# Last stage of a graph network on one core: message rows fetched once per step instead of once per tile of edges

## The chip, the core and the metric

The program runs on one core of one Trainium2 chip. The metric is the device time of one execution in microseconds (us), without the profiler. Five engines work side by side: TensorE (PE in the profile, its weight loads PEld), VectorE (DVE), ScalarE (ACT), GpSimd (POOL) and SyncE (SP). [...]

## What is computed

Two graph layers over 6250 nodes of 256 features and 100,000 edges, which come sorted by their target `dst`. Cut to what matters:

```python
h = relu(layernorm(x))
x = x + L0(h, src, dst, ...)          # attention over edges, then an MLP per node
h = relu(layernorm(x))
all_msg = einsum('nf,rfo->rno', h, weight)          # one message per node and relation, 16 relations
msg  = all_msg[rel_type, src] * norm                # one row of 256 per edge
gate = sigmoid(einsum('nf,rf->rn', h, gate_weight[..., 0])[rel_type, src])
agg  = segment_sum(msg * gate[:, None], dst, num_segments=6250)
x = x + relu(agg)
```

The change is about `msg` and `segment_sum`: one row of 256 numbers for each edge is fetched from the table of messages and added to its target node.

## The kernel before

**Stages.** `prepare` computes the steps' tables, q, k and v, and fills the first 221 us. `attention` (to 1710 us) gathers q and v rows edge by edge. `node_mlp` and `messages` (to 2550 us) are the dense part; `messages` writes `msg_d`, 16 rows of 256 per node, already gated. `edge_sum` is the last stage, and `finish` adds x and stores.

**Tiles and steps.** 128 edges make a tile of edges (782 of them, and one of padding, `DENSE` = 783), 128 nodes a tile of nodes (`NODE_TILES` = 49). Since edges are sorted by target, a tile of edges belongs to one tile of nodes, or to two where it spans their border. A **step** is one pair of the two; there are `STEPS` = 832. So a border tile of edges has two steps, one for each tile of nodes.

**The last stage before** (`edge_sum`, L1257 to L1341). The order is written out by hand, unrolled; nothing schedules it.
- GpSimd gathers: for each tile of edges one indirect DMA (L1294) of 128 rows of 1 KB from `msg_d`, by a column of the index table `msg_i`, into a ring of 64 places (`RING`). Before a place is used again it waits for `summed`, the count of finished steps, to be at least e - 64 + 50, because the program doesn't know which steps read the tile. Every fourth gather it waits also for `landed` (L1292).
- SyncE relays landings (L1280 to L1282): the twenty semaphores `got` tell of landings one by one; SyncE waits for each in turn and adds one to `landed`.
- TensorE, for each step (L1302 to L1314): it loads from the table `place` the number of the tile of edges that the step reads, makes the ring's address from it in registers, waits for the one-hot matrix and for `landed` to reach that number (a register's value), and multiplies the one-hot matrix (128x128, float32) with the 128x256 rows. The load is issued two steps ahead. In the profile one such multiplication is two matmuls.
- VectorE, for each step: the one-hot matrix (L1326), which holds the edge's weight where the target matches, in a ring of four; and the addition of the step's product to `sums` (L1339), two steps later, at an address that it loads eight at a time from `place` (L1331).

**The index table.** `prepare` finds for each step its tile of edges by a product: `cols` holds src, dst, relation and weight of the edges (columns n = 0 to 3 in that order, each with two PSUM banks), `sel` selects. The line L748 does it in seven chunks c of edge tiles, for n = 0, 1 and 3. The message index 16 * src + relation was made on the columns before the product (L427), for tiles of edges, and seven transposes (L756) turn it into `msg_i` (L451, L452). `src_i`, which the attention stage uses, is by step.

Of the kernel before, what the change touches and what calls it, by code (L numbers as in the profile page):

```python
# [20 lines left out]
I32 = mybir.dt.int32  # L21
U16 = mybir.dt.uint16
U_ROUND = float(3 * 2 ** 22)
ALU = mybir.AluOpType
# [3 lines left out]
P = 128  # L28
# [61 lines left out]
def gnn_program(nc, x, src, dst, rel, norm, wqkv, bqkv, g_attn, b_attn, g_res, b_res,  # L90
# [17 lines left out]
    msg_i_d = dram("msg_i_d", [P, EDGE_TILES_PAD], I32)  # L108
    tab_d = dram("tab_d", [ROUNDS, TABLE], U16)

    with ExitStack() as whole:
# [35 lines left out]
        msg_i = sb(last, "msg_i_again", [P, EDGE_TILES_PAD], I32)  # L147
# [47 lines left out]
def prepare(nc, sb, ps, sem, x, src, dst, rel, norm, wqkv, bqkv, g_attn, b_attn, iota_n, ident, ident_b, part, ones,  # L195
# [20 lines left out]
    with ExitStack() as ctx:  # L216
        dloc = sb(ctx, "dloc", [P, STEPS])
        norm_s = sb(ctx, "norm_s", [P, STEPS])
        msg_i = sb(ctx, "msg_i", [P, EDGE_TILES_PAD], I32)
# [78 lines left out]
        with nc.Block() as block:  # L298
            @block.vector
            def _(dve):  # L300
# [121 lines left out]
                for c in range(ICN):  # L422
                    if c >= 2:
                        dve.wait_ge(sel_free, c - 1)
                    if c == 2:
                        dve.wait_ge(split, 3)
                        nc.vector.scalar_tensor_tensor(out=cols[:, 2], in0=cols[:, 0], scalar=float(RELS), in1=cols[:, 2],  # L427
                                                       op0=ALU.mult, op1=ALU.add).then_inc(split, 1)
# [21 lines left out]
                at["src"] = signal(last)  # L450
                nc.vector.tensor_copy(msg_i[:, 0:4 * IC], pb[4][:, 0:4 * IC])  # L451
                at["msg"] = signal(nc.vector.tensor_copy(msg_i[:, 4 * IC:], pb[5][:, 0:(ICN - 4) * IC]))  # L452
# [255 lines left out]
            def _(pe):  # L708
# [34 lines left out]
                for c in range(ICN):  # L743
                    pe.wait_ge(dve_did, at["sel", c])
                    for n in (0, 1, 3):
                        for h in range(2):
                            for part_of in (cols_hi, cols_lo):
                                mm = nc.tensor.matmul(pb[2 * n + h][:, 0:SH], part_of[:, n, c, :],  # L748
                                                      sel[:, c % 2, h * SH:(h + 1) * SH],
                                                      start=(c == 0 and part_of is cols_hi),  # L750
                                                      stop=(c == ICN - 1 and part_of is cols_lo))
                    mm.then_inc(sel_free, 1)
                    if c == ICN - 3:
                        pe.wait_ge(split, 4)
                        for d in range(ICN):
                            nc.tensor.transpose(pb[4 + d // 4][:, d % 4 * IC:(d % 4 + 1) * IC], cols[:, 2, d], ident[0:IC, 0:IC])  # L756
# [500 lines left out]
def edge_sum(nc, sb, ps, sem, table, sums, iota_n, late, place, msg_i, idx_ld, late_ld, x1_d, x1_all, got):  # L1257
# [3 lines left out]

    before = [16 * len([n for n in range(STEPS) if n % SLOTS // 2 == b]) for b in range(len(got))]
    BANKS = 4
    HOTS = 4
    RING = 64
    x1_ld, hot_ok, summed, acc_ok, zero_ok, landed = (
        sem(f"rel_{n}") for n in ("x1", "hot", "sum", "acc", "zero", "landed"))
    with ExitStack() as ctx:
        dloc, norm_s = late[:, 0], late[:, 1]
        rows = sb(ctx, "rel_rows", [P, RING * FEAT])  # L1270
# [3 lines left out]
        with nc.Block() as block:  # L1274
            @block.sync
            def _(sp):
                for g in range(GROUPS):
                    sp.dma_start(x1_all[:, g], x1_d.rearrange("(g t p) f -> g p t f", t=GROUP, p=P)[g]).then_inc(x1_ld, 16)
                for e in range(DENSE):
                    b = e % len(got)  # L1280
                    sp.wait_ge(got[b], before[b] + 16 * (e // len(got) + 1))
                    sp.sem_inc(landed, 1)  # L1282
                sp.wait_ge(x1_ld, 16 * GROUPS)

            @block.gpsimd
            def _(pool):
                pool.wait_ge(idx_ld, 16)
                for e in range(DENSE):
                    if e >= RING:
                        pool.wait_ge(summed, e - RING + NODE_TILES + 1)  # L1290
                    if e >= len(got) and e % 4 == 0:
                        pool.wait_ge(landed, e - len(got) + 4)  # L1292
                    at = (e + 1) % RING * FEAT
                    nc.gpsimd.indirect_dma_start(rows[:, at:at + FEAT], None, table,  # L1294
                                                 bass.IndirectOffsetOnAxis(ap=msg_i[:, e:e + 1], axis=0)
                                                 ).then_inc(got[e % len(got)], 16)

            @block.tensor
            def _(pe):
                def edge_of(n):  # L1300
                    r, s = n // UNROLL, n % UNROLL
                    return nc.values_load_multi_w_load_instructions(  # L1302
                        place[r:r + 1, s:s + 1], engines=[mybir.EngineType.PE], min_val=1, max_val=DENSE,
                        skip_runtime_bounds_check_because="the tile of edges that a step reads, counted from one")[1][0]

                pe.wait_ge(late_ld, 48)
                ahead = [edge_of(0), edge_of(1)]
                for n in range(STEPS):
                    edge = ahead.pop(0)
                    at = nc.s_assert_within(pe.snap(edge & (RING - 1)) * FEAT, 0, (RING - 1) * FEAT,  # L1310
                                            skip_runtime_bounds_check_because="the remainder of a division by the ring's length")
                    pe.wait_ge(hot_ok, n + 1)
                    pe.wait_ge(landed, edge)
                    nc.tensor.matmul(sum_ps[n % BANKS][:], hot[:, n % HOTS, :], rows[:, bass.ds(at, FEAT)],  # L1314
                                     start=True, stop=True).then_inc(summed, 1)
                    if n + 2 < STEPS:
                        ahead.append(edge_of(n + 2))
# [704 lines left out]
```

## Time and profile before

| | us |
|---|---|
| median of 3 timed runs | 3281.6 |
| lowest, highest | 3278.4, 3282.5 |
| the profiled execution, its own span | 3773.2 |
| first stage ends | 221.4 |
| attention ends | 1710 |
| messages are done, first gather of the last stage | 2550 |
| last addition ends | 3748.4 |

The profile is of one execution, recorded by the hardware; its span is the time that it knows of it, and no other time of that execution is given. "Busy" is time in which an engine executes. Idle time is put down to what released the engine: an instruction of another engine, a DMA, or "issue", where the profile shows nothing that was waited for. Register, branch and semaphore instructions are of an engine's sequencer (PEldq, SPq, DVEq) and don't count as busy. PEclk is the granted TensorE clock, 1.00 for 2.4 GHz.

### The profile page before, as it was taken

What the parts mean: (1) busy time and instruction counts of PE and PEld (TensorE: products, weight loads), DVE (VectorE), ACT (ScalarE), POOL (GpSimd) and SP (SyncE); (2) the same over time, 40 slices, a digit from 0 to 9 for tenths busy, and PEclk for the clock granted to TensorE, in tenths of its full rate; (3) what the DMA queues carried; (4) which work ended last, traced back from release to release, by engine and by line L of the source; (5) the groups of instructions that cost most, each with busy time, mean ns of one, the idle gap of its engine ahead of it and who ended that gap; (6) DMA issues with size and microseconds to landing.
All of it is one profiled execution on the core that took longest, in us unless ns stands there. A gap on an engine that the chain in (4) does not pass through costs nothing. (4 is left out here: it accounts for less than half of the span.)

```text
span 3773.2 us, 52431 instructions
## 1 busy us (share of the span) xinstructions
PE 2896.0 (77%) x13207; PEld 1940.5 (51%) x13207; DVE 2133.7 (57%) x4604; ACT 963.3 (26%) x2525; POOL 1732.1 (46%) x1863
## 2 busy tenths in 40 slices
PE   6838888888888888869999999992655555555555
PEld 4525555555555555549998888871333333333332
DVE  6727776677767777768862222222544444444446
ACT  3513333333333333346663333330000000000000
POOL 2555655555555555433300000006466666666661
PEclk9968998899989999979999999995867677776678
DMA  4455666666666666533345444445233333333332
GB/s 151 147 166 164 196 192 193 181 192 189 194 188 190 192 191 195 160 114 99 99 136 210 187 186 188 187 178 164 69 91 92 92 92 92 91 91 92 92 92 88
DMA packets 233908, 557.07 MB, mean 148 GB/s; under 512 B 48498, under 2 KB 128454, under 8 KB 221095
## 3 DMA queue, kind: packets, MB, share of 16 engines
q0 software_dynamic: 104144, 324.24, 30.4%
q1 hardware_dynamic: 108463, 193.61, 14.1%
q10 hardware_dynamic: 21032, 35.85, 3.2%
q8 instruction: 141, 2.31, 0.2%
q14 instruction: 128, 1.05, 0.1%
HBM read 402.87 MB, written 150.71 MB: 147 GB/s over the span
## 5 line engine op out<-in xcount | busy, mean ns | idle before, releaser
L1294 POOL DMA_INDIRECT rel_rows<-msg_d,msg_i_again x783 | 743.3, 949 | 976.8 <-ACTq L1274 571.7
L1314 PE MATMUL rel_ps<-rel_rows,rel_hot 128*128 x1664 | 678.5, 538 | 525.0 <-issue 364.4
L873 POOL DMA_INDIRECT qv_rows<-qv_d,src_i x832 | 798.4, 960 | 567.6 <-PE out_ps L1155 354.2
L1314 PEld LDWEIGHTS rel_ps<-rel_rows,rel_hot 128*128 128x128 f32 x1664 | 367.1, 254 | 836.5 <-issue 806.3
L1339 DVE TENSOR_TENSOR sums_all<-sums_all,rel_ps 128x256 f32 x832 | 350.4, 421 | 630.4 <-PE rel_ps L1314 247.0
L1155 PE MATMUL out_ps<-qv_rows,hot 128*128 128x264 f32 x1664 | 635.8, 467 | 44.8 <-DVE qv_rows L950 25.0
L1031 ACT COPY at_acc<-out_ps 128x264 f32 x832 | 310.3, 380 | 726.9 <-PE out_ps L1155 581.1
L1110 PE MATMUL kx<-k,hot_t 128*128 x2496 | 398.4, 297 | 64.4 <-issue 48.4
L896 DVE TENSOR_TENSOR qv_rows<-qv_rows,kx 128x512 f32<-128x512 f32 x416 | 278.7, 679 | 204.4 <-remote 121.6
L1957 PE MATMUL up_hid_ps<-up_split,ms_hTs 128*128 128x512 f32 x1416 | 347.5, 396 | 0.0
L1110 PEld LDWEIGHTS kx<-k,hot_t 128*128 128x128 bf16 x2496 | 252.9, 105 | 175.4 <-issue 108.6
L1155 PEld LDWEIGHTS out_ps<-qv_rows,hot 128*128 128x128 f32 x1664 | 277.3, 209 | 87.1 <-issue 63.7
L1326 DVE TENSOR_SCALAR rel_hot<-iota_n,late 128x128 f32<-128x128 f32 x832 | 297.2, 357 | 0.1
L1957 PEld LDWEIGHTS up_hid_ps<-up_split,ms_hTs 128*128 128x128 f32 x1416 | 264.7, 189 | 59.9
L1165 PEld LDWEIGHTS out_ps<-at_zero 1*128 1x128 bf16 x832 | 76.2, 92 | 377.9 <-issue 366.0
L950 DVE TENSOR_TENSOR qv_rows<-qv_rows,p_ps 128x1056 f32<-128x1056 f32 x208 | 250.5, 1246 | 0.4 <-PE p_ps L1144 0.3
L901 DVE TENSOR_REDUCE sc<-qv_rows 128x32 f32<-128x1024 f32 x208 | 248.3, 1215 | 1.8
L1957 PE MATMUL up_out_ps<-up_split,ms_hTs 128*128 128x512 f32 x936 | 233.6, 397 | 0.0
L1165 PE MATMUL out_ps<-at_zero 1*128 1x8 bf16 x832 | 145.8, 175 | 108.1 <-issue 61.8
L1957 PEld LDWEIGHTS up_out_ps<-up_split,ms_hTs 128*128 128x128 f32 x936 | 174.9, 189 | 39.5
L1736 PE MATMUL up_out_ps<-wout,up_split 128*128 128x256 f32 x1176 | 154.8, 290 | 22.8 <-DVE up_x_h L1503 22.7
L1736 PEld LDWEIGHTS up_out_ps<-wout,up_split 128*128 128x128 f32 x1176 | 147.5, 196 | 26.0 <-DVE up_x_h L1503 15.0
(213 smaller groups left out, 2883.3 us busy)
## 6 DMA issues: line engine op xcount, KB each, us to landing
msg_d<-up_x SPq DMA_DIRECT2D x33, 1024.0 KB, 3.9
msg_d<-up_gelu SPq DMA_DIRECT2D x33, 1024.0 KB, 3.8
msg_d<-up_res SPq DMA_DIRECT2D x32, 1024.0 KB, 3.8
dl_b<-dlt_d ACTq DMA_DIRECT2D x50, 512.0 KB
qv_rows<-qv_d,src_i POOLq DMA_INDIRECT x832
rel_rows<-msg_d,msg_i_again POOLq DMA_INDIRECT x783
qv_d<-qv SPq DMA_DIRECT2D x6, 1820.0 KB, 7.2
agg_d<-at_acc SPq DMA_DIRECT2D x49, 132.0 KB
```

Source lines behind the costliest of these rows:

```text
L873: nc.gpsimd.indirect_dma_start(rows[:, n % SLOTS, :], None, qv_d, bass.IndirectOffsetOnAxis(ap=src_i[:, n:n + 1], axis=0)).then_inc(got[n ...
L896: nc.vector.tensor_tensor(q, q, kx[i % 2][:], ALU.mult).then_inc(prod_ok, 1)
L950: nc.vector.tensor_tensor(v, v, weights.to_broadcast([P, QUAD, HEADS, HW]), ALU.mult).then_inc(val_ok, 1)
L1031: nc.scalar.copy(acc[:, at:at + AGGW], out_ps[:, bass.ds(banks[s % QUAD], AGGW)]).then_inc(acc_ok, 1)
L1110: last = nc.tensor.matmul(kx[i % 2][:, b, :], hot_t[:, k % HOT_RING, s * P:(s + 1) * P], k_flat[:, bass.ds(tiles[s] * KW + n * FEAT, FEAT) ...
L1155: nc.tensor.matmul(out_ps[:, bass.ds(bank, AGGW)], hot[:, s, :], rows[:, slot(k, s), FEAT:], start=False, stop=True, skip_group_check=True ...
L1294: nc.gpsimd.indirect_dma_start(rows[:, at:at + FEAT], None, table, bass.IndirectOffsetOnAxis(ap=msg_i[:, e:e + 1], axis=0)).then_inc(got[e ...
L1314: nc.tensor.matmul(sum_ps[n % BANKS][:], hot[:, n % HOTS, :], rows[:, bass.ds(at, FEAT)], start=True, stop=True).then_inc(summed, 1)
L1326: nc.vector.tensor_scalar(hot[:, n % HOTS, :], iota_n[:], dloc[:, n:n + 1], norm_s[:, n:n + 1], ALU.is_equal, ALU.mult).then_inc(hot_ok, 1)
L1339: nc.vector.tensor_tensor(sums[:, bass.ds(here, FEAT)], sums[:, bass.ds(here, FEAT)], sum_ps[n % BANKS][:], ALU.add).then_inc(acc_ok, 1)
L1736: last = nc.tensor.matmul(out_ps[n_t % 2], hid[:, a, m, t * P:(t + 1) * P], wout[:, b, m, :], start=(i == 0), stop=(i == len(parts) - 1))
L1957: last = nc.tensor.matmul(mm_ps[m % BANKS][:], hTs[:, n % 2, a, k, :], wrel[:, c, b, k], start=(i == 0), stop=(i == len(parts) - 1))
```

## The change

Rows are gathered for each step instead of each tile of edges: 832 gathers in place of 783, so that step n reads place n % 40. The ring has 40 places with one semaphore per two, as in the attention stage. GpSimd waits for `summed` to be n - 39. SyncE's relay and the semaphore `landed` go. TensorE waits for two gathers before every second step, with fixed numbers, and loads nothing and computes no address. The index is now made by step: L748 also chooses the relation (n = 2, its high part alone, since it is a small whole number), and 16 * src + relation is made afterwards by VectorE from `src_i`. The transposes and the multiplication at L427 go. VectorE's part of the last stage, its load of places included, and the table `place` stay.

```diff
--- before.py
+++ after.py
@@ -105,7 +105,7 @@
     hb_d = dram("hb_d", [STEPS, P])
     fl_d = dram("fl_d", [ICN * HEADS, 2 * FLAGS])
     late_d = dram("late_d", [2, P, STEPS])
-    msg_i_d = dram("msg_i_d", [P, EDGE_TILES_PAD], I32)
+    msg_i_d = dram("msg_i_d", [P, STEPS], I32)
     tab_d = dram("tab_d", [ROUNDS, TABLE], U16)
 
     with ExitStack() as whole:
...
@@ -422,10 +422,6 @@
                 for c in range(ICN):
                     if c >= 2:
                         dve.wait_ge(sel_free, c - 1)
-                    if c == 2:
-                        dve.wait_ge(split, 3)
-                        nc.vector.scalar_tensor_tensor(out=cols[:, 2], in0=cols[:, 0], scalar=float(RELS), in1=cols[:, 2],
-                                                       op0=ALU.mult, op1=ALU.add).then_inc(split, 1)
                     at["sel", c] = did(nc.vector.tensor_scalar(sel[:, c % 2], edge_tile[0:IC, :], part_c[0:IC, c:c + 1], None,
                                                                ALU.is_equal))
                     if c == 1:
@@ -447,9 +443,12 @@
                 dve.wait_ge(pe_did, 5)
                 for h in range(2):
                     last = nc.vector.tensor_copy(src_i[:, h * SH:(h + 1) * SH], pb[h][:, 0:SH])
-                at["src"] = signal(last)
-                nc.vector.tensor_copy(msg_i[:, 0:4 * IC], pb[4][:, 0:4 * IC])
-                at["msg"] = signal(nc.vector.tensor_copy(msg_i[:, 4 * IC:], pb[5][:, 0:(ICN - 4) * IC]))
+                at["src"] = did(last)
+                for h in range(2):
+                    a, b = h * SH, (h + 1) * SH
+                    last = nc.vector.scalar_tensor_tensor(out=msg_i[:, a:b], in0=src_i[:, a:b], scalar=float(RELS),
+                                                          in1=pb[4 + h][:, 0:SH], op0=ALU.mult, op1=ALU.add)
+                at["msg"] = signal(last)
                 for h in range(2):
                     a, b = h * SH, (h + 1) * SH
                     last = nc.vector.scalar_tensor_tensor(out=dloc[:, a:b], in0=node_tile[:, a:b], scalar=-float(P),
@@ -742,18 +741,15 @@
                 pe.wait_ge(split, 3)
                 for c in range(ICN):
                     pe.wait_ge(dve_did, at["sel", c])
-                    for n in (0, 1, 3):
+                    for n in range(4):
+                        parts_of = (cols_hi,) if n == 2 else (cols_hi, cols_lo)
                         for h in range(2):
-                            for part_of in (cols_hi, cols_lo):
+                            for i, part_of in enumerate(parts_of):
                                 mm = nc.tensor.matmul(pb[2 * n + h][:, 0:SH], part_of[:, n, c, :],
                                                       sel[:, c % 2, h * SH:(h + 1) * SH],
-                                                      start=(c == 0 and part_of is cols_hi),
-                                                      stop=(c == ICN - 1 and part_of is cols_lo))
+                                                      start=(c == 0 and i == 0),
+                                                      stop=(c == ICN - 1 and i == len(parts_of) - 1))
                     mm.then_inc(sel_free, 1)
-                    if c == ICN - 3:
-                        pe.wait_ge(split, 4)
-                        for d in range(ICN):
-                            nc.tensor.transpose(pb[4 + d // 4][:, d % 4 * IC:(d % 4 + 1) * IC], cols[:, 2, d], ident[0:IC, 0:IC])
                 pe.wait_ge(sel_free, ICN)
                 pe.sem_inc(pe_did, 1)
 
@@ -1259,15 +1255,15 @@
 
 
 
+    PER = 2
+    RING = PER * len(got)
     before = [16 * len([n for n in range(STEPS) if n % SLOTS // 2 == b]) for b in range(len(got))]
     BANKS = 4
     HOTS = 4
-    RING = 64
-    x1_ld, hot_ok, summed, acc_ok, zero_ok, landed = (
-        sem(f"rel_{n}") for n in ("x1", "hot", "sum", "acc", "zero", "landed"))
+    x1_ld, hot_ok, summed, acc_ok, zero_ok = (sem(f"rel_{n}") for n in ("x1", "hot", "sum", "acc", "zero"))
     with ExitStack() as ctx:
         dloc, norm_s = late[:, 0], late[:, 1]
-        rows = sb(ctx, "rel_rows", [P, RING * FEAT])
+        rows = sb(ctx, "rel_rows", [P, RING, FEAT])
         hot = sb(ctx, "rel_hot", [P, HOTS, P])
         sum_ps = [ps(ctx, f"rel_ps{i}", [P, FEAT]) for i in range(BANKS)]
 
@@ -1276,45 +1272,27 @@
             def _(sp):
                 for g in range(GROUPS):
                     sp.dma_start(x1_all[:, g], x1_d.rearrange("(g t p) f -> g p t f", t=GROUP, p=P)[g]).then_inc(x1_ld, 16)
-                for e in range(DENSE):
-                    b = e % len(got)
-                    sp.wait_ge(got[b], before[b] + 16 * (e // len(got) + 1))
-                    sp.sem_inc(landed, 1)
                 sp.wait_ge(x1_ld, 16 * GROUPS)
 
             @block.gpsimd
             def _(pool):
                 pool.wait_ge(idx_ld, 16)
-                for e in range(DENSE):
-                    if e >= RING:
-                        pool.wait_ge(summed, e - RING + NODE_TILES + 1)
-                    if e >= len(got) and e % 4 == 0:
-                        pool.wait_ge(landed, e - len(got) + 4)
-                    at = (e + 1) % RING * FEAT
-                    nc.gpsimd.indirect_dma_start(rows[:, at:at + FEAT], None, table,
-                                                 bass.IndirectOffsetOnAxis(ap=msg_i[:, e:e + 1], axis=0)
-                                                 ).then_inc(got[e % len(got)], 16)
+                for n in range(STEPS):
+                    if n >= RING:
+                        pool.wait_ge(summed, n - RING + 1)
+                    nc.gpsimd.indirect_dma_start(rows[:, n % RING, :], None, table,
+                                                 bass.IndirectOffsetOnAxis(ap=msg_i[:, n:n + 1], axis=0)
+                                                 ).then_inc(got[n % RING // PER], 16)
 
             @block.tensor
             def _(pe):
-                def edge_of(n):
-                    r, s = n // UNROLL, n % UNROLL
-                    return nc.values_load_multi_w_load_instructions(
-                        place[r:r + 1, s:s + 1], engines=[mybir.EngineType.PE], min_val=1, max_val=DENSE,
-                        skip_runtime_bounds_check_because="the tile of edges that a step reads, counted from one")[1][0]
-
-                pe.wait_ge(late_ld, 48)
-                ahead = [edge_of(0), edge_of(1)]
                 for n in range(STEPS):
-                    edge = ahead.pop(0)
-                    at = nc.s_assert_within(pe.snap(edge & (RING - 1)) * FEAT, 0, (RING - 1) * FEAT,
-                                            skip_runtime_bounds_check_because="the remainder of a division by the ring's length")
+                    if n % PER == 0:
+                        b = n % RING // PER
+                        pe.wait_ge(got[b], before[b] + 16 * PER * (n // RING + 1))
                     pe.wait_ge(hot_ok, n + 1)
-                    pe.wait_ge(landed, edge)
-                    nc.tensor.matmul(sum_ps[n % BANKS][:], hot[:, n % HOTS, :], rows[:, bass.ds(at, FEAT)],
+                    nc.tensor.matmul(sum_ps[n % BANKS][:], hot[:, n % HOTS, :], rows[:, n % RING, :],
                                      start=True, stop=True).then_inc(summed, 1)
-                    if n + 2 < STEPS:
-                        ahead.append(edge_of(n + 2))
 
             @block.vector
             def _(dve):
```

TensorE in the last stage, two steps of before and five of now. `rel_ps` is the bank of the product, `rel_rows` the ring, `rel_hot` the one-hot matrix; `rel_landed` is the relay's count, `got` counts landings. Before:

```order
L1302 TENSOR_LOAD place
L1314 REGISTER_ALU [waits rel_landed,rel_hot]
L1314 ISA
L1314 MATMUL rel_ps3<-rel_rows,rel_hot 128x256
L1302 TENSOR_LOAD place
L1314 REGISTER_ALU [waits rel_landed,rel_hot]
L1314 ISA
L1314 MATMUL rel_ps0<-rel_rows,rel_hot 128x256
```

Now:

```order
L1294 MATMUL rel_ps1<-rel_rows,rel_hot 128x256 [waits rel_hot]
L1294 MATMUL rel_ps2<-rel_rows,rel_hot 128x256 [waits rel_hot,got17]
L1294 MATMUL rel_ps3<-rel_rows,rel_hot 128x256 [waits rel_hot]
L1294 MATMUL rel_ps0<-rel_rows,rel_hot 128x256 [waits rel_hot,got18]
L1294 MATMUL rel_ps1<-rel_rows,rel_hot 128x256 [waits rel_hot]
```

The register load and the two register instructions of each step are gone, and their waits stand at the matmul itself, with a landing's semaphore at every second one.

GpSimd at the start of the last stage, before (the pattern of one gather with the wait for `landed` and three without goes on, from the 65th gather on with `rel_sum` at every one):

```order
L1285 UNCONDITIONAL_BRANCH [waits barrier_Pool_Activation_PE_DVE_SP_gather]
L1294 DMA rel_rows<-msg_d,msg_i_again 128x256 [waits rel_idx]
L1294 DMA rel_rows<-msg_d,msg_i_again 128x256 x19
L1294 DMA rel_rows<-msg_d,msg_i_again 128x256 [waits rel_landed]
L1294 DMA rel_rows<-msg_d,msg_i_again 128x256 x3
L1294 DMA rel_rows<-msg_d,msg_i_again 128x256 [waits rel_landed]
L1294 DMA rel_rows<-msg_d,msg_i_again 128x256 x3
```

Now:

```order
L1277 UNCONDITIONAL_BRANCH [waits barrier_Pool_Activation_PE_DVE_SP_gather]
L1283 DMA rel_rows<-msg_d,msg_i_again 128x256 [waits rel_idx]
L1283 DMA rel_rows<-msg_d,msg_i_again 128x256 x39
L1283 DMA rel_rows<-msg_d,msg_i_again 128x256 [waits rel_sum] x792
L1270 UNCONDITIONAL_BRANCH
```

40 gathers start without a wait for the sums, then each of the other 792 waits for `rel_sum`; no gather waits for `rel_landed`.

## Rows read from the trace of the kernel before

**Rows 1.** Busy time by stage; columns stand in the first row.

```profile
core 0: us, PE busy (x) PEld busy (x) DVE busy (x) ACT busy (x) POOL busy (x), PEclk, DMA share, GB/s
0.00:221.40 221.40, 175.77 (x605) 107.12 (x605) 153.62 (x479) 100.80 (x255) 89.34 (x131) 0.96 0.44 144
221.40:1710.00 1488.60, 1210.12 (x6609) 752.39 (x6610) 1038.73 (x1697) 500.92 (x1382) 836.48 (x877) 0.89 0.64 181
1710.00:2550.00 840.00, 831.56 (x4331) 713.89 (x4329) 361.72 (x757) 361.60 (x889) 63.03 (x73) 1.00 0.43 166
2550.00:3748.50 1198.50, 678.51 (x1664) 367.10 (x1664) 565.87 (x1665) 0.00 (x0) 743.28 (x783) 0.71 0.32 92
```

**Rows 2.** The page: costliest groups of the last stage.

```profile
L1294 POOL DMA_INDIRECT rel_rows<-msg_d,msg_i_again x783 | 743.3, 949 | 976.8 <-ACTq L1274 571.7
L1314 PE MATMUL rel_ps<-rel_rows,rel_hot 128*128 x1664 | 678.5, 538 | 525.0 <-issue 364.4
...
L1339 DVE TENSOR_TENSOR sums_all<-sums_all,rel_ps 128x256 f32 x832 | 350.4, 421 | 630.4 <-PE rel_ps L1314 247.0
...
L1326 DVE TENSOR_SCALAR rel_hot<-iota_n,late 128x128 f32<-128x128 f32 x832 | 297.2, 357 | 0.1
```

**Rows 3.** One line, the gather (L1294): durations (ns min/median/max), idle time by releaser.

```profile
L1294 POOL DMA_INDIRECT rel_rows<-msg_d,msg_i_again x783: 943/949/1037, 2550.1 to 3697.5; - x196
...
  issue: 194.0, 554
  PE rel_ps L1314: 132.6, 175
  remote: 76.0, 50
```

**Rows 4.** Timeline, start of the gathers (start us, us, engine, line, idle before).

```profile
2550.05 1.04 POOL L1294 DMA_INDIRECT rel_rows<-msg_d,msg_i_again  x1 [571.73 <-ACTq L1274]
2551.39 0.95 POOL L1294 DMA_INDIRECT rel_rows<-msg_d,msg_i_again  x1 [0.30 <-issue]
...
2552.65 0.95 POOL L1294 DMA_INDIRECT rel_rows<-msg_d,msg_i_again  x1 [0.30 <-issue]
```

**Rows 5.** Timeline, GpSimd alone, end of the gathers.

```profile
3696.22 0.95 POOL L1294 DMA_INDIRECT rel_rows<-msg_d,msg_i_again  x1 [0.31 <-issue]
3697.48 0.95 POOL L1294 DMA_INDIRECT rel_rows<-msg_d,msg_i_again  x1 [0.30 <-issue]
```

**Rows 6.** One line, the matmuls (L1314) and their register work, whole stage.

```profile
L1314 PEldq ALU_OP  x832: 2/32/1384, 2565.1 to 3746.8; - x167
```

**Rows 7.** The same line, 3700 to 3750 us alone, no gather left.

```profile
L1314 PE MATMUL rel_ps<-rel_rows,rel_hot x116: 379/392/478, 3699.8 to 3747.3; 128*128 x116
L1314 PEldq ALU_OP  x57: 32/32/32, 3700.3 to 3746.8; - x57
```

**Rows 8.** SyncE, the relay (L1282), 2565 to 3697 us.

```profile
L1282 SPq EVENT_SEMAPHORE  x780: 3/17/711, 2565.0 to 3696.4; - x195
```

**Rows 9.** VectorE, the places loaded every eighth step (L1331).

```profile
L1331 DVEq TENSOR_LOAD <-place x104: 1823/1876/1941, 2562.8 to 3741.5; - x104
```

**Rows 10.** The page: gathers of the attention stage.

```profile
L873 POOL DMA_INDIRECT qv_rows<-qv_d,src_i x832 | 798.4, 960 | 567.6 <-PE out_ps L1155 354.2
```

**Rows 11.** First stage, the choosing matmuls (L748).

```profile
L748 PE MATMUL prep_ps<-sel,cols_hi x42: 352/352/684, 28.6 to 47.5; 112*128 112x416 f32 x42
```

**Rows 12.** Timeline of the first stage, the transposes and what follows.

```profile
42.64 0.83 PE L756 MATMUL prep_ps<-ident,k 112*128 112x112 f32 x7
...
47.48 0.35 PE L748 MATMUL prep_ps<-sel,cols_hi 112*128 112x416 f32 x1
...
47.67 0.35 PE L748 MATMUL prep_ps<-sel,cols_lo 112*128 112x416 f32 x1
...
49.15 0.61 DVE L451 CAST msg_i<-prep_ps 128x448 int32<-128x448 f32 x1
...
49.68 0.50 DVE L452 CAST msg_i<-prep_ps 128x336 int32<-128x336 f32 x1
```

More of the change, by code:

```diff
@@ L146, in gnn_program @@
         last = whole.enter_context(ExitStack())
-        msg_i = sb(last, "msg_i_again", [P, EDGE_TILES_PAD], I32)
+        msg_i = sb(last, "msg_i_again", [P, STEPS], I32)
         late = sb(last, "late", [P, 2, STEPS])
@@ L218, in prepare @@
         norm_s = sb(ctx, "norm_s", [P, STEPS])
-        msg_i = sb(ctx, "msg_i", [P, EDGE_TILES_PAD], I32)
+        msg_i = sb(ctx, "msg_i", [P, STEPS], I32)
         dlt = sb(ctx, "dlt", [P, ICN, P], BF16)
```

## The prediction

> **What bounds the kernel now.** First the busy time by stage [rows 1]: the last stage takes 1198.5 us of the 3773.2 us span. In it GpSimd is busy 743.3 us, TensorE 678.5 us and VectorE 565.9 us: no engine is full, so a wait or an overhead sets the pace. The stage before it has TensorE busy 831.6 of 840.0 us, and there is no slack in it. Then the page's groups [rows 2]: 783 gathers of 949 ns, 1664 matmuls (two a step, 832 steps), 832 additions of 421 ns and 832 one-hots of 357 ns.
>
> The gather's own line [rows 3] has some 405 us idle between gathers. Part of it comes with every gather: where nothing holds GpSimd up, gathers still start 1.25 us apart, 0.95 us busy and 0.30 us not [rows 4, 5]. That is 235 us over 782 gaps. From 2550.05 to 3697.48 us are 1147.4 us, 782 x 1.25 are 977.5; so **170 us** are waits. Who made them? When the last gather starts at 3697.5 us, 116 matmuls, 58 steps, are still to come [rows 5, 7], and they take 47.5 us, 0.82 us a step, with the granted clock high. GpSimd had run as far ahead as its ring lets it: in this execution TensorE was behind, not the gathers. Yet with no gather running its step is 0.82 us, far below the 1.25 us of a gather. What slows it beside gathers is in its register work: an operation that takes 32 ns each time in the last 47 us [rows 7] takes up to 1384 ns over the stage [rows 6], and SyncE's relay goes from 17 to 711 ns at its worst [rows 8].
>
> **Profiled and unprofiled time.** The span is 3773.2 us, the median of the runs is 3281.6: 491.6 us less. So stretches of this trace do not exist at that length in a timed run, and the question of this case is which. The third stage is packed and can give nothing [rows 1]. If the last stage took its 1198.5 us in a timed run too, the first would have to give up all its 45.6 us without a matmul (221.4 - 175.8) and the attention stage nearly all the 449.9 us in which VectorE is not busy (1488.6 - 1038.7): 495.5 in sum, against 491.6 wanted. No stage with chains of waits runs that tight. I conclude that the last stage gives up a good part. The natural part is the 170 us: register and semaphore operations that stretch many times over, on two engines, only while gathers run, look like the recording of events in a crowd, not like work.
>
> **The change part by part, in a timed run.**
> - Gathers: 832 instead of 783, since a tile of edges that spans two node tiles is fetched twice. If the gathers set the pace, it costs 49 periods. GpSimd's busy time alone gives 49 x 0.949 = 46.5 us, the lower bound; the whole period gives 49 x 1.25 = 61.3 us, the upper one, if the 0.30 us are real. Nothing in the trace tells how much of the 0.30 us a timed run keeps; I take the middle, **+54 us**. The attention gathers have the same durations [rows 10]. The transfers grow by 6% from a DMA share of 0.32 [rows 1]: nothing. The Trainium skill, page "DMA: Bandwidth & Descriptors", section "Anatomy of one DMA — SWDGE (gpsimd) path", calls descriptor generation small, with many descriptors to be had before it shows; by that the 49 gathers would cost nothing. The trace speaks against it: each holds GpSimd for 949 ns.
> - TensorE loses a register load, two register operations and a wait in every step, and SyncE loses 784 relays. Their cover is the gather: 0.82 us a step with all of them [rows 7] against 0.949 us at least for a gather. Removed, they are worth nothing while gathers set the pace; without that cover they are worth the 170 us and what follows from them.
> - The ring. GpSimd is no longer held 14 steps behind (64 less 50) but always 40, and doesn't wait for landings. The first gather starts at 2550.05 us and TensorE's first register operation at 2565.1 us [rows 4, 6]; landing takes less than that, 12 gathers. 40 cover it. TensorE now waits for pairs: at most one more gather, 1.25 us, once. After the last gather I allow 5 us for landing, two matmuls and an addition: 0, as before.
> - VectorE still loads its places from a table every eighth step, 1.88 us each [rows 9]. It is unchanged and its pace is in the 0.82 us.
> - First stage: 14 more choosing matmuls at 0.19 us apart [rows 12] (their own 352 ns overlap [rows 11]) are +2.7 us; seven transposes go, -0.8 us [rows 12]. VectorE's two operations that make the message index stay two, 0.61 and 0.50 us, now reading src_i as well; one multiplication further up goes and was hidden. All this lies before the first products: **+2 us**, between 0 and +4.
>
> Sum: +54 + 2 = **+56 us**, 3281.6 + 56 = 3337.6 us. Against the profiled execution the sum is another one, and shows what I mean: 831 x 1.25 = 1038.8 after 2550.05, 5 behind it, ends the stage at 3593.9 in place of 3748.5, with +2 a span near **3621 us**. I expect the profile's span to fall by about 150 us while the time rises.
>
> **The rivals.**
> 1. Faster: the stretched operations are real. Mechanism: TensorE's and SyncE's register and semaphore operations become slow while gathers run, the ring fills, GpSimd waits. The change takes most of them away. In full that gives 3281.6 - 155 + 2 = 3128.6 us. For it: all 170 us stand in the trace, and TensorE is idle for "issue" [rows 2]. Against it: the account of the 491.6 us above. A share s of it gives 56 - 209 s us, no change at s = 0.27 (46 us of real waits), 3233 at half. In a sentence of its own: the Trainium skill, "Runtime: NRT & Kernel Launch", section "The launch sequence", gives profile and run a gap of about 6 us whatever the kernel, by which the stretches would be real and this rival right; here the gap is 491.6 us, so the trace does not bear the rule out. Chance 0.28.
> 2. No change: a timed gather is shorter than VectorE's and TensorE's 0.82 us a step, in profile and out of it. Then the 49 gathers are hidden and 3284 us result. Against it: it needs 949 ns of busy time to shrink by 14% while VectorE's doesn't. This also covers a cancelling share of rival 1. Chance 0.11.
> 3. Slower than forecast: the 40 deep ring or pairs make TensorE wait at its landings; by one 1.25 us for each time the ring starts cold, so a few us. It widens the upper end only.
>
> That the change doesn't do what it says can be left out: its gathers and their addresses are fixed numbers.
>
> **How the numbers follow.** Forecast, gathers set the pace: 0.61, all of it slower; its own range is 3327 (46.5 and 0 less 1) to 3350 (61.3, 4 and a few us of rival 3). Rival 2: 0.11 within 0.2% (6.6 us, about what a measurement of this kernel tells from no change). Rival 1: 0.28 faster. The range takes in the forecast, rival 2 and rival 1 down to half its price, 3233, and a little below: 3230 to 3350.
>
> **What would show it.** In the profile after: 832 gathers starting 1.25 us apart with hardly a longer gap, the last one near 3589 us; GpSimd at 66% or more of the stage; TensorE waiting for landed rows; no 700 ns stretches on TensorE; a stage of some 1044 us. Those would hold with a rise or a fall of the time. What tells them apart is the time alone: below 3275 us the register work was a real bound. If gathers in the new profile still wait for TensorE, the reading of the stretched operations is wrong.

## The result and the profile after

The change makes the kernel **slower: 3340.64 us** (4 runs, 3338.56 to 3342.85) against 3280.49 us before, a ratio of 1.0185 with a 95% interval of 1.0173 to 1.0197, or +60.2 us. The forecast was 3337.6 us.

The trace shown ahead of the prediction can't be understood without one fact, which the experiments brought out: the kernel before takes near 3280 us in some series of runs and near 3800 us in others, steadily within each, and its recorded execution of 3773.2 us was of the second kind, its timed runs of the first ("at 3280" and "at 3800" below; each difference is taken within one series).

Busy time by stage of the kernel after, at 3280 (columns as in [rows 1]):

```profile
0.00:219.90 219.90, 171.98 (x612) 105.72 (x612) 153.10 (x478) 100.91 (x255) 89.03 (x130) 0.98 0.45 145
219.90:1425.00 1205.10, 1109.78 (x6604) 710.48 (x6605) 1025.48 (x1696) 503.44 (x1381) 831.58 (x877) 0.96 0.76 224
1425.00:2265.70 840.70, 832.21 (x4336) 714.54 (x4335) 362.38 (x758) 362.27 (x891) 63.60 (x74) 1.00 0.44 166
2265.70:3313.60 1047.90, 758.45 (x1664) 435.17 (x1664) 574.66 (x1664) 0.00 (x0) 789.49 (x832) 0.63 0.38 111
```

The last stage takes 1047.9 us; the attention stage's gathers end at 1298 us where they ended at 1584 in the trace before, at 3800, in code that the change does not touch. The page's groups (as [rows 2]):

```profile
L1283 POOL DMA_INDIRECT rel_rows<-msg_d,msg_i_again x832 | 789.5, 949 | 825.1 <-ACTq L1270 571.7
L1294 PE MATMUL rel_ps<-rel_rows,rel_hot 128*128 128x256 f32 x1664 | 758.6, 603 | 295.3 <-DMA rel_rows<-msg_d,msg_i_again 271.1
...
L1317 DVE TENSOR_TENSOR sums_all<-sums_all,rel_ps 128x256 f32 x832 | 350.4, 421 | 471.3 <-PE rel_ps L1294 460.9
...
L1304 DVE TENSOR_SCALAR rel_hot<-iota_n,late 128x128 f32<-128x128 f32 x832 | 294.6, 354 | 0.1
```

And the gather's own line (as [rows 3]; the last row is the time from a gather's start to its landing):

```profile
L1283 POOL DMA_INDIRECT rel_rows<-msg_d,msg_i_again x832: 945/949/1037, 2265.7 to 3307.6; - x167
...
  issue: 143.0, 469
  PE rel_ps L1294: 110.4, 362
...
DMA to landing us min/median/max: 2.6/2.7/6.2
```

832 gathers lie between 2265.7 and 3307.6 us: 1041.9 us over 831 gaps, 1.254 us each. The idle time of 143.0 and 110.4 us is 253.4 in all, 0.305 us a gap: nothing but the 0.30 us that come with each gather. Not one gap is long. A row lands 2.7 us after its gather starts. The timeline of the end shows who waits for whom now:

```profile
3305.08 0.94 POOL L1283 DMA_INDIRECT rel_rows<-msg_d,msg_i_again  x1 [0.30 <-PE rel_ps L1294]
...
3305.34 2.08 PE L1294 MATMUL rel_ps<-rel_rows,rel_hot 128*128 128x256 f32 x4 [0.44 <-DMA rel_rows<-msg_d,msg_i_again]
...
3306.33 0.94 POOL L1283 DMA_INDIRECT rel_rows<-msg_d,msg_i_again  x1 [0.30 <-issue]
...
3307.58 0.95 POOL L1283 DMA_INDIRECT rel_rows<-msg_d,msg_i_again  x1 [0.30 <-PE rel_ps L1294]
...
3311.65 2.07 PE L1294 MATMUL rel_ps<-rel_rows,rel_hot 128*128 128x256 f32 x4 [1.01 <-DMA rel_rows<-msg_d,msg_i_again]
...
3313.86 0.42 DVE L1317 TENSOR_TENSOR sums_all<-sums_all,rel_ps 128x256 f32 x1 [0.43 <-PE rel_ps L1294]
```

TensorE waits for landed rows ("DMA" as the releaser) and works four matmuls, two steps, at a time, as the pairs of its waits have it; 6.7 us pass from the last gather's start to the end of the last addition. I had allowed 5.

### The profile page after: what moved, and what is told of

It reads as the page before. It is cut to its first block and busy times, and to the rows that moved or that the text cites. A ratio compares the mean times of both kernels' runs of the same rounds, so it can differ in the third digit from the quotient of the medians.

```text
span 3336.8 us, 48617 instructions
## 1 busy us (share of the span) xinstructions
PE 2872.5 (86%) x13214; PEld 1965.9 (59%) x13214; DVE 2129.7 (64%) x4603; ACT 966.6 (29%) x2525; POOL 1773.7 (53%) x1912
## 5 line engine op out<-in xcount | busy, mean ns | idle before, releaser
L1283 POOL DMA_INDIRECT rel_rows<-msg_d,msg_i_again x832 | 789.5, 949 | 825.1 <-ACTq L1270 571.7
L1294 PE MATMUL rel_ps<-rel_rows,rel_hot 128*128 128x256 f32 x1664 | 758.6, 603 | 295.3 <-DMA rel_rows<-msg_d,msg_i_again 271.1
L1294 PEld LDWEIGHTS rel_ps<-rel_rows,rel_hot 128*128 128x128 f32 x1664 | 435.2, 289 | 618.4 <-DMA rel_rows<-msg_d,msg_i_again 527.3
L1151 PE MATMUL out_ps<-qv_rows,hot 128*128 128x264 f32 x1664 | 590.1, 437 | 33.0 <-DVE qv_rows L946 18.5
L1106 PE MATMUL kx<-k,hot_t 128*128 x2496 | 354.4, 278 | 13.2 <-DVE hot_t L885 7.3
L1151 PEld LDWEIGHTS out_ps<-qv_rows,hot 128*128 128x128 f32 x1664 | 251.6, 191 | 75.7 <-issue 54.3
L1106 PEld LDWEIGHTS kx<-k,hot_t 128*128 128x128 bf16 x2496 | 235.4, 98 | 99.0 <-issue 37.6
```

The lines of the kernel that those rows point to most:

```text
L1106: last = nc.tensor.matmul(kx[i % 2][:, b, :], hot_t[:, k % HOT_RING, s * P:(s + 1) * P], k_flat[:, bass.ds(tiles[s] * KW + n * FEAT, FEAT) ...
L1151: nc.tensor.matmul(out_ps[:, bass.ds(bank, AGGW)], hot[:, s, :], rows[:, slot(k, s), FEAT:], start=False, stop=True, skip_group_check=True ...
L1283: nc.gpsimd.indirect_dma_start(rows[:, n % RING, :], None, table, bass.IndirectOffsetOnAxis(ap=msg_i[:, n:n + 1], axis=0)).then_inc(got[n ...
```

## The experiments

All edits are to the kernel before, but for E5. Two series came at 3280 (that of the result and that of E7, E8 and E9), three at 3800 (E1 to E4; E5 and E6; E10 to E12). The record has chip 4 beside E5 and E6 at 3800 and beside E7 to E9 at 3280, so the chip's number alone doesn't tell which it will be.

**E1, before once more.** No edit.

> The kernel before, unchanged, recorded once more. Two accounts of the 491.6 us between its span and its timed runs. Theory A: that one recording was disturbed (a property of the execution, not of the kernel): now the span is near 3280 us, the attention stage some 284 us shorter as in the profile of the change, and the gathers of the last stage start 1.25 us apart all through. Theory B: recording this kernel always stretches its register work: the span is again above 3600 us and TensorE's register operations again take up to 1400 ns.

It fell at 3800: the recorded execution took 3791.84 us, its own span 3790.0 of them, beside a median of 3800.7 for runs of the same kernel. So a recorded execution is a timed one, 1.8 us longer than its span. The other runs, at 3280 and at 3800, have spans on record too, 1.8 to 1.9 us shorter than their times: recording stretched nothing. What theory B foresaw came (a span of 3790.0 us, a register operation of 1421 ns), but not for its reason, and theory A was wrong. The 491.6 us lie between two conditions in which the kernel runs, and in the slow one each execution has them. Stages and gathers are as in the trace ahead of the prediction:

```profile
0.00:217.50 217.50, 172.06 (x605) 105.03 (x605) 153.91 (x479) 100.81 (x255) 89.40 (x131) 0.98 0.45 147
217.50:1720.00 1502.50, 1219.81 (x6661) 757.03 (x6662) 1045.02 (x1717) 505.54 (x1395) 837.40 (x882) 0.89 0.63 180
1720.00:2552.00 832.00, 823.54 (x4279) 706.28 (x4277) 354.12 (x738) 355.51 (x876) 59.51 (x70) 1.00 0.44 167
2552.00:3764.50 1212.50, 672.30 (x1664) 372.48 (x1664) 564.69 (x1664) 0.00 (x0) 741.49 (x783) 0.71 0.31 91
```

```profile
L1294 POOL DMA_INDIRECT rel_rows<-msg_d,msg_i_again x783: 940/946/1036, 2552.0 to 3713.2; - x196
...
  issue: 192.9, 549
  PE rel_ps L1314: 134.1, 176
  remote: 88.9, 52
```

**E2 and E10, the first stage alone.**

```diff
+++ prepare as in the change, msg_i [P, STEPS]; edge_sum as before, reading msg_i[:, e]
```

> The first stage of the change, with the last stage of before. The rows of the last stage are chosen by the wrong column of the index, so the messages added are not those of the reference; the amount of work is the same. My step for the first stage was +2 us, 0 to +4. If it holds, this kernel is 0 to 4 us slower than before, and the last stage alone answers for 56 to 60 of the 60.1 us. A rival: the waits behind the choosing products (src_i, then the index, then the first products) cost 8 us or more, and the gathers correspondingly less.

> The first stage of the change with the last stage of before (the wrong column of the index is read, so the messages added are not those of the reference; the amount of work is the same). In the profile of the change the first gather of the last stage starts at 2265.7 us, in those of before's front 2263.8 and 2264.9. My step was +2 us; a rival is 0, its cover being the wait for loads. Where before takes near 3280 us I expect +1 to +4 us, close to what five rounds can tell. Its last stage is that of before, so its profile shows before's gathers on such a chip: 1.25 us apart, none longer.

Both came at 3800: -0.5 us (0.9995, interval 0.9983 to 1.0007) and +3.5 us (1.0007, 0.9994 to 1.0021). By the times the first stage costs nothing that can be told; 8 us or more at once are not excluded by the second alone (its interval ends at +8.0), but are by the first (+2.7). The traces tell more. The last choosing matmul starts at 47.67 us in the trace before [rows 12] and here in the change:

```profile
48.66 0.34 PE L748 MATMUL prep_ps<-sel,cols_lo 112*128 112x416 f32 x1
```

That is +0.99 us in one pair of executions, and executions of the same first stage differ by up to 1.9 us at this point. The fourteen traces together are clearer. From the first to the last choosing matmul pass 17.9 to 19.4 us in the ten with the first stage of before (18.7 in the mean) and 20.1 to 21.1 in the four with that of the change (20.6): +1.9 us. The first gather of the attention stage starts 2.0 us later in the mean, at 220.8 in place of 218.8 us, though single ones overlap there.

**E3, E6 and E11, no register work on TensorE.**

```diff
-                    edge = ahead.pop(0)
-                    at = nc.s_assert_within(pe.snap(edge & (RING - 1)) * FEAT, ...
+                    edge = min(DENSE, n + 1 - n * NODE_TILES // STEPS)
+                    at = edge % RING * FEAT
```

> The kernel before with TensorE's table load, registers and address left out: the tile of edges that a step reads is a fixed number spread evenly over the steps, so some steps read a neighbouring tile and the sums are not the reference's. 783 gathers, SyncE's relay and the ring stay. If the gathers set the pace, the time is that of before within 4 us (at most the few us that before loses to waits). If the register work was a bound that the change removed, this kernel is clearly faster than before, by 20 us or more.

> The kernel before with TensorE's table load, registers and address left out, some steps reading a neighbouring tile, as once before; there it was 16 us faster where before took 3800 us, with 79 of 782 gaps between gathers still long. Where before takes near 3280 us: gathers set the pace, so it is 0 to 4 us faster. If register work were the bound, 20 us or more.

> The kernel before without TensorE's table load, registers and register address (some steps read a neighbouring tile), a third time, for a chip on which before takes near 3280 us; on the other it gained 16 to 18 us. If gathers set the pace it gains nothing, under 4 us. If register work is a bound in part, 10 us or more.

All three came at 3800: -16.3 us (ratio 0.9959, 0.9946 to 0.9973), -17.9 (0.9957, 0.9939 to 0.9974) and -13.8 (0.9958, 0.9946 to 0.9971). That is between the two marks of the expectation (4 and 20 us). So there the register work has a price, a tenth of the waits. Most of them stay without it: 167 us of 782 gaps beyond 1.254 us in E3, as many as in the trace before (167) and 14 less than in E1 (181). And yet no step's matmul is late in E3: none starts more than 0.43 us after its one-hot is made and the second matmul of the step before has started, where in the trace before 198 of 830 start more than 0.5 us after that. What makes GpSimd wait must be sought elsewhere (E5). At 3280 this edit was not tried. E8 answers for it from the other side.

**E4 and E7, 49 more gathers.**

```diff
+                    if e % 16 == 8:
+                        if e > 8:
+                            pool.wait_ge(spare_ld, 16 * (e // 16))
+                        nc.gpsimd.indirect_dma_start(spare[:], None, table, ...).then_inc(spare_ld, 16)
```

> The kernel before with 49 more gathers, one behind every sixteenth, of rows that nobody reads; nothing waits for them but the end. If the gathers set the pace and the 0.30 us between them are real, +61 us (49 x 1.25), as much as the whole change. If only the 0.949 us of busy time are paid, +46. If the gathers were hidden behind 0.82 us steps, 0 to 10 us.

> The kernel before with 49 more gathers of rows that nobody reads, once more (60.7 us where before took 3800 us). Where before takes near 3280 us: +61 us if gathers set the pace with their whole 1.25 us period, +46 if only the 0.949 us of busy time count, 0 to 10 us if they are hidden behind TensorE's register work.

At 3800 +60.7 us (1.0164, 1.0151 to 1.0178), at 3280 +65.5 us (1.0194, 1.0180 to 1.0208). E7 adds as many gathers as the change (and a wait behind each, long met) and nothing else of it, and gets the change's whole loss. At 3800 the waits stay beside the added gathers (185 us in E4 and 181 in E1 beyond 1.254 us a gap). The extra gather (L1302) stands in the row of the others with the same 1.25 us (timeline, GpSimd alone, E7):

```profile
2275.01 0.94 POOL L1296 DMA_INDIRECT rel_rows<-msg_d,msg_i_again  x1 [0.30 <-issue]
2276.26 0.95 POOL L1302 DMA_INDIRECT rel_spare<-msg_d,msg_i_again  x1 [0.30 <-issue]
2277.51 0.95 POOL L1296 DMA_INDIRECT rel_rows<-msg_d,msg_i_again  x1 [0.30 <-issue]
```

Rival 2, gathers hidden behind 0.82 us steps, falls with this: 65.5 us for 49 are 1.34 us each, a little over the period of 1.25. So does, for gathers like these, what the Trainium skill says on the page "DMA: Bandwidth & Descriptors", section "Anatomy of one DMA — SWDGE (gpsimd) path", that many descriptors can be made before their cost shows.

**E5, the change once more**, beside before.

> The change, unaltered, beside the kernel before on the same chip. Where before takes near 3280 us: 3340 us, +60, with gathers 1.25 us apart. Where before takes near 3800 us, as in the last four comparisons, two theories part. Theory A: what is slow there is TensorE's and SyncE's supply of instructions while gathers run; the change takes SyncE's 784 relays and half of TensorE's instructions away, its gathers come 1.25 us apart again, and it is 100 us or more faster than before. Theory B: something else is slow there, which the change leaves; then the 170 us of waits stay and the change is about 60 us slower there too.

It came at 3800: 3807.37 us against 3798.73, +8.6 us (1.0025, 1.0012 to 1.0037). Neither theory: the change wins most of its gathers back there, but not the 170 us. The gather's line:

```profile
L1283 POOL DMA_INDIRECT rel_rows<-msg_d,msg_i_again x832: 940/946/1037, 2563.3 to 3750.6; - x167
...
  issue: 171.0, 541
  PE rel_ps L1294: 160.3, 247
  remote: 69.7, 43
```

832 gathers take 1187.3 us; over 1.254 a gap that leaves 145 us of waits, where the trace before has 167 and E1 181 by the same count. Its timeline shows what they are made of:

```profile
3007.14 0.42 DVE L1317 TENSOR_TENSOR sums_all<-sums_all,rel_ps 128x256 f32 x1 [2.88 <-PE rel_ps L1294]
3007.48 0.34 DVE L1304 TENSOR_SCALAR rel_hot<-iota_n,late 128x128 f32<-128x128 f32 x1
3007.66 0.98 POOL L1283 DMA_INDIRECT rel_rows<-msg_d,msg_i_again  x1 [0.30 <-issue]
...
3007.87 1.22 PE L1294 MATMUL rel_ps<-rel_rows,rel_hot 128*128 128x256 f32 x2 [2.27 <-issue]
3008.94 0.94 POOL L1283 DMA_INDIRECT rel_rows<-msg_d,msg_i_again  x1 [0.30 <-issue]
3011.36 0.42 DVE L1317 TENSOR_TENSOR sums_all<-sums_all,rel_ps 128x256 f32 x1 [3.54 <-remote]
3011.50 0.94 POOL L1283 DMA_INDIRECT rel_rows<-msg_d,msg_i_again  x1 [1.61 <-remote]
3011.70 0.34 DVE L1304 TENSOR_SCALAR rel_hot<-iota_n,late 128x128 f32<-128x128 f32 x1
...
3012.18 1.19 PE L1294 MATMUL rel_ps<-rel_rows,rel_hot 128*128 128x256 f32 x2 [3.09 <-DVE rel_hot L1304]
3014.19 0.42 DVE L1317 TENSOR_TENSOR sums_all<-sums_all,rel_ps 128x256 f32 x1 [2.16 <-PE rel_ps L1294]
3014.33 0.94 POOL L1283 DMA_INDIRECT rel_rows<-msg_d,msg_i_again  x1 [1.90 <-PE rel_ps L1294]
```

TensorE is not late here. Its pairs of matmuls start at 3007.87 and 3012.18 us, 0.05 and 0.14 us after their one-hots are made, and over the whole stage none starts more than 0.43 us late, counted as in E3. Late is the sign that a step is finished. Counted in order, the addition at 3011.36 is that of step 275 (the first is 0). By the trace the two matmuls of this step ended at 3003.67; such ends are modelled, but those of steps 276 and 277 had started by 3007.87. 379 of 830 additions start more than 0.5 us after their product and VectorE's work before it, by up to 5.2 us; in the change at 3280 it is 83, by up to 1.7 us, beside 104 loads of places. GpSimd sees the same: its gather at 3011.50 waits for the same step 275 in the same count `summed`, and starts 0.14 us after the addition, as the gather at 3014.33 does after the addition of step 276. Of the 90 gathers from the 41st on that start after more than 0.6 us of idle time, 86 start 0.14 us after the addition of their step, 4.3 us in the median after its product. In the trace before it is 87 of 92.

So at 3800 the count that TensorE raises with its matmuls is seen microseconds late, by two engines at the same moment, and the one-hots, which VectorE makes behind its additions, and TensorE's next matmuls come late in consequence. This is so with register operations on TensorE and without. Whether the matmul ends late or its signal does, and why, is open. That the gathers themselves slow it fits the end of the stage [rows 7], where they are over, but no run took them away.

**E8 and E9, more register work on TensorE.**

```diff
-                        ahead.append(edge_of(n + 2))
+                        ahead.append([edge_of(n + 2) for _ in range(2)])       # E9: range(4)
...
+                    for other in more:
+                        pe.wait_ge(hot_ok, other)
```

> The kernel before with TensorE's work on registers enlarged: two table loads for each step instead of one, and one more wait on the value, which is always met. In 3700 to 3750 us of the profile of before a step takes 0.82 us with one load; a second of 0.29 us plus a wait of 0.05 makes at most 1.16 us. A step has 783 x 1.25 / 832 = 1.18 us. If gathers set the pace where before takes 3280 us: no change, under 7 us. If register work is a bound: +250 us at the most (832 x 0.3), over 50 in any case. Where before takes 3800 us, TensorE's instructions are slow beside gathers, and it is slower by 50 us or more.

> The same with four table loads for each step. One load takes 0.29 us and a wait 0.05: a step of TensorE's takes 0.68 to 0.82 us plus 3 x 0.34, so 1.7 to 1.84 us against the 1.18 us of the gathers. The cover is gone and TensorE sets the pace: +430 to +550 us. If loads overlap each other, less: with 0.1 us a load, it stays below 1.18 us and costs nothing.

Both at 3280. E8 (the loads double, and one more wait that is always met): 3276.04 us against 3277.27, -1.2 us (0.9996, 0.9987 to 1.0005), no change. With twice the loads of before nothing is lost. It is also the best picture of before at 3280 that I have, since its 783 gathers and its relay are those of before. First the last stage (columns as in [rows 1]), then the gather's line, then a register operation of TensorE's:

```profile
2263.80:3249.50 985.70, 730.72 (x1664) 319.45 (x1664) 587.85 (x1665) 0.00 (x0) 742.28 (x783) 0.77 0.38 112
```

```profile
L1294 POOL DMA_INDIRECT rel_rows<-msg_d,msg_i_again x783: 942/947/1037, 2263.8 to 3243.4; - x196
...
  issue: 188.3, 618
  PE rel_ps L1316: 49.1, 161
```

```profile
L1316 PEldq ALU_OP  x832: 32/32/32, 2278.8 to 3247.1; - x167
```

783 gathers from 2263.8 to 3243.4 us are 979.6 us, 1.253 us a gap. No gap is long, and 32 ns are 32 ns at minimum, median and maximum (in E7 too, with TensorE's code as before), against 2 to 1384 in [rows 6]. The last stage takes 985.7 us, 62.2 less than the change's.

E9: 3843.59 us, +566.3 us (1.1724, 1.1708 to 1.1740), a little over the 430 to 550 expected. Four loads of 0.29 us each do not overlap (one step's start at 3000.22, 3000.58, 3000.93 and 3001.29 us), and now GpSimd waits for TensorE. First the gather's line, then the loads:

```profile
L1294 POOL DMA_INDIRECT rel_rows<-msg_d,msg_i_again x783: 940/944/1036, 2264.7 to 3699.6; - x196
...
  PE rel_ps L1316: 654.5, 697
...
  issue: 31.8, 79
```

```profile
L1302 PEldq TENSOR_LOAD <-place x3328: 280/290/320, 2264.1 to 3814.0; - x196
```

The matmuls' 832 steps lie between 2279.9 and 3816.2 us, 1.85 us a step. The gathers' cover for TensorE ends somewhere between two and four loads.

**E12, half the rows.**

```diff
-                    nc.gpsimd.indirect_dma_start(rows[:, at:at + FEAT], None, table, ... ap=msg_i[:, e:e + 1]
+                    nc.gpsimd.indirect_dma_start(rows[0:64, at:at + FEAT], None, table, ... ap=msg_i[0:64, e:e + 1]
```

> The kernel before, each gather of the last stage fetching 64 rows instead of 128 (the other half of the ring is zeroed once, so half of the messages are left out of the sums). It measures what the 1.25 us consist of. Theory A: the 0.95 us are written per row and the 0.30 us per gather: period 0.78 us, then VectorE's and TensorE's 0.82 us a step are the bound, the stage takes 832 x 0.82 = 682 instead of 980 us, 300 us faster. Theory B: the whole is per gather: no change. Where before takes 3800 us the gain of A is smaller.

At 3800: +2.8 us (1.0012, 0.9998 to 1.0025). The time can't tell much there, since waits fill what is saved (GpSimd is idle 454 us between gathers, 421 in E1), but the row can:

```profile
L1294 POOL DMA_INDIRECT rel_rows<-msg_d,msg_i_again x783: 892/899/982, 2558.1 to 3717.2; - x196
```

899 ns for 64 rows, 946 for 128 (E1): 47 ns for 64 rows, and by an estimate along this line some 850 that come with every gather. Theory A is wrong, B nearly right.

## Why the prediction was right, and where its reasoning was not

- **Gathers set the pace in a timed run** (forecast 0.61): right, at 3280. Every gap is 1.25 us in the change and in E8, and TensorE waits for landings.
- **49 gathers, 46.5 to 61.3 us, taken as 54**: the upper end was the true one. 49 x 1.254 are 61.4, and the 0.30 us between gathers are real, as all of the span is (E1). The middle was no evidence; E7 has 65.5. I also weighed the Trainium skill's small price of descriptors (the page and section named at E4 and E7) against the 949 ns of the row and took the row, rightly.
- **Register load, registers and relay worth nothing under that cover**: right at 3280; E8 doubles the load for -1.2 us. (SyncE's relays are 783, not 784.) At 3800 the registers alone are worth 14 to 18 us (E3, E6, E11).
- **First stage, +2 us**: borne out by the traces, +1.9 us for the choosing products as in the sum (2.7 - 0.8) and 2.0 to the first gather; E2 and E10 don't tell it from 0.
- **Sum**: 61.4 + 1.9 = 63.3 us against 60.2 measured, whose interval is 56.8 to 64.6. My 56 was short by the part of the gathers' period that I left out.
- **The account of the 491.6 us**: the step that failed. I set it down to the recording, where the two came from different conditions (E1). The Trainium skill, page "Runtime: NRT & Kernel Launch", section "The launch sequence", has a gap of about 6 us, the same for every kernel, by which the profile's time is the longer. That it doesn't depend on the kernel agrees: it is 1.8 to 1.9 us in every run here. Its size and sign don't agree: here the run is longer than the span (3338.56 against 3336.8), though the page's total may take in more than the span. So the stretches were real in their execution, as I had said the rule would have it. That the last stage is shorter in the timed runs, which I had worked out from the 491.6 us, was right (985.7 us in E8 against 1198.5), and so the waits rightly got no price; the reason I gave for them was wrong. That this did no harm was luck: the change was measured in the same series as the timed runs at 3280 (three of the result's four runs of before are those ahead of the prediction), while at 3800 the difference is +8.6 us (E5), and nothing in my reasoning foresaw that.
- **What slows TensorE's step beside gathers**: I put it on the register work. Without that work most of the waits stay (E3), and the late count of finished steps is there in E5 without a register operation on TensorE.
- **The profile of the change**: forecast near 3621 us of span, last gather at 3589; it has 3336.8 and 3307.6. The stage's length was forecast as 1044 us and is 1048. The rest is the attention stage, which in the other condition gathers at 1.64 us a step instead of 1.30.
- **Rival 1** (0.28): wrong at 3280; at 3800 nearly what I had priced as its break-even. There the change keeps +61.4 us of gathers. Beside the trace before it gets back 22 us of waits (167 - 145) and 17 behind the last gather (to the end of the last addition 51.0 us before, 33.6 after), +22 us in the stage. Beside E1 it is 35 and 18 us, +8 in the stage. These are single executions; the measured difference of the medians is +8.6. A kernel judged in that condition alone would have been called the same.

No run tried a version that might beat both. At 3280, with the register work hidden, before already gathers as few tiles as there are, at the pace of the gathers.

## What to carry to other kernels

Compare the recorded execution with the timed runs before reading it. Where they differ by more than a few us, look for unchanged stages that run at another pace, and record again before any sum. A queue of indirect gathers is priced by their number: here 1.25 us each with 128 rows, and some 50 ns less with 64; keep their count low and let other engines pay in registers, as long as a step of theirs stays below the gathers' period. To find out how much register work fits under such a cover, add some: one load more cost nothing, three cost 566 us.

## What the hardware showed that I had not expected

- The same kernel takes 3277 to 3281 us in some series and 3799 to 3801 in others (medians), a factor of 1.16. Gathers and VectorE's operations keep their durations. In stages with gathers TensorE's register and SyncE's semaphore operations of 17 to 46 ns take up to 1.4 us (E1), and the count of finished steps is seen late, by up to 5.2 us at the additions, by VectorE and GpSimd at once (E5). In the dense stage between, nothing differs (840.7 us in the change at 3280, 840.0 in the trace before at 3800; E1's row of 832.0 has its border set later, with 52 matmuls fewer).
- A gather's time hardly depends on its rows (899 ns for 64, 946 for 128) nor on their width. The attention stage's rows have 520 numbers where the last stage's have 256, and they take the same 949 ns in the kernel after:

```profile
L869 POOL DMA_INDIRECT qv_rows<-qv_d,src_i x832: 943/949/1239, 219.9 to 1298.3; - x167
```

- With that, 1664 gathers at 1.25 to 1.30 us fill 2120 of the change's 3337 us: at 3280 the attention stage, too, goes nearly at the pace of its gathers.
